# Bf16 norms, f16 feed-forward halves and new instruction orders in an attention kernel with six local layers

## The chip, the cores and the metric

One core of a Trainium2 chip runs the whole program. The metric is the device time of one execution in microseconds (us), as the median of three runs. TensorE (PE) multiplies matrices, VectorE (DVE), ScalarE (ACT) and GpSimd (POOL) work elementwise, SyncE (SP) issues all the DMAs.

## What is computed

The input is 8 batches of 512 tokens with 128 channels, in float32. First comes one causal attention with 16 heads of 64 (norm, projections, softmax over all earlier tokens, output projection, gated residual). Then six layers of local attention and feed-forward follow, of which this is the core:

```python
def attn_layer(x, Wqkv, qs, ksc, Wo):
    q, k, v = split(x @ Wqkv); q = l2norm(q) * qs; k = l2norm(k) * ksc
    q = q * cos * scale + rotate_half(q) * sin * scale      # k with 1 / scale
    out = local_attention(q, k, v)                            # windows of 32, and the window before
    return out @ Wo
def ffn_layer(x, g, bln, W1, b1, W2, b2):
    xn = (x - mu) / sqrt(var + 1e-05) * g + bln
    a, gate = split(xn @ W1 + b1)                             # 341 columns each
    return a * gelu(gate) @ W2 + b2
for i in range(6):
    x = attn_layer(shift_tokens(x), ...) + x
    x = ffn_layer(shift_tokens(x), ...) + x
```

## The kernel before, in words

The causal stage (lines L539 and the like) takes the first 670 us or so and is left almost as it is. The local stage works through 48 units, one for each layer and batch (m = 8 * layer + batch). A unit has two halves of eight heads each, v = 2m and 2m + 1. Everything is channels by tokens, 128 x 512 per tile; two such tiles side by side make a 128x1024 PSUM tile, and there are four of those: psA0, psA1, psB0 and psB1.

The steps of one half, by their names in the code: `pj` (4 of them, c = 0 to 3) projects q or k: six f16 matmuls, since x and the weights are each kept as a high and a low f16 half and three products are added. `sq` (ACT, L985) squares it, `tc` and `ts` (DVE, L1237 and L1245) multiply it by the rotary tables, `ad` (POOL, L1349 and L1350) adds these crosswise into a tile h, of which there are HN = 5, `qa` (POOL, L1354) adds the squares of the two halves of the head dimension. `ss` sums the squares over the partitions with four matmuls. The norm's inverse is made by `nr` and `ns` (ACT, L990 to L1001) and `nw` (POOL, L1357 to L1361), one Newton step on a Ln/Exp estimate. `bc` (k = 0, 1) spreads that factor to all partitions of a head by two f32 matmuls of 32 rows, `bm` (DVE, L1253) multiplies h by it, and `dm` (SP, L486) issues four DMAs for each of the four tiles, to qf and kf. `vp`, `ve` (ACT, L1007) and `vd` (SP, L502 and L504) make and copy the values. `sc` (rp = 0, 1 and t = 0 to 3) makes scores by 16 small matmuls (64 rows, 32 columns of the array), `mx` (DVE, L1257) takes their maximum, `ng` subtracts it on PE by two bf16 matmuls, `ex` (ACT, L1015) exponentiates, `tp` (L732) transposes by eight f32 matmuls, `te` (ACT, L1022) copies, `pv` (32 small matmuls each) applies them to the values, `nm` (DVE, L1266 and L1270) divides, `ot` (L758), `oe` (ACT, L1029) and `ol` (DVE, L1228) transpose and split into f16 halves.

Once a unit: `op` (24 f16 matmuls) and `rs` (DVE) are the output projection and its residual; `la`, `lb` (one f32 matmul each) with `lq`, `lw`, `lr` (ACT), `ln` (DVE) and `lx` (POOL, L1364 to L1368) are the layer norm; `f` (j = 0 to 2) is W1, two f32 matmuls of 512 columns each; `ge` (ACT, L1057) is gelu, `fm` (DVE, L1301) the product with the gate, `fo` W2 as three f32 matmuls, `fr` (DVE, L1308 and L1310) the residual with the bias b2. `xh` and `xl` split x for the next projection. Weights come once a layer (`st`, `wh`, `wl`, `oh`, `ow`; `feed_of` for W1 and W2, `tb` for the rotary tables).

Each engine works through its steps strictly in the order that the strings TENSOR, SCALAR, VECTOR, GPSIMD and SYNC write out for one unit; `walk` unrolls them, where "+1" takes a step one unit further ahead and ":A" or ":B" picks the pair of PSUM tiles. A step waits for the steps named in its code (`done`, `all_done`), and a step that takes a PSUM tile waits until the last reader of the tile's last use is through (`take`, LAST). The Gelu and the Ln/Exp functions of ACT are in different tables; `local_scalar` loads a table (L953) where a step needs another than the last one did.

## Time and profile before

| | |
|---|---|
| median of 3 runs | 3932.62 us (3932.16 to 3944.91) |
| the profiled execution's own time | 3944.91 us, the highest of the three |
| span of the profiled execution | 3944.5 us |
| busy: PE, its weight loads, DVE, ACT, POOL | 94%, 54%, 76%, 61%, 59% |
| mean granted TensorE clock | 0.983 of 2.4 GHz |

A row of the timeline gives start, duration, engine, line, operation, output<-inputs and count. Matmuls are pipelined, so what a PE step costs is the time from its start to the start of the next step and not the duration. An f32 matmul leaves two records, so "x4" of f32 is two matmuls. L677 is the helper by which nearly all local matmuls are recorded, so PE steps are told apart by their tiles.

### The profile page before, as it was taken

The numbers are of one execution on the slowest core, as the hardware profiler recorded it, in microseconds if no ns is written. First come the engines' busy times: TensorE is split into PE (matmuls) and PEld (weight loads), VectorE is DVE, ScalarE is ACT, GpSimd is POOL, SyncE is SP. The second block draws the span as 40 slices with busy tenths as digits, with TensorE's granted clock in tenths as the row PEclk, the third lists the DMA queues.
The fourth block names the chain that finished last, engine by engine and source line by source line (L and its number), as shares of the span: only waits on it lengthen the run. The fifth ranks groups of instructions, "written<-read, shape, count | busy, mean of one in ns | idle before, by whom it ended". The sixth has DMA issues, their size and how long they took to land.

```text
span 3944.5 us, 165118 instructions
## 1 busy us (share of the span) xinstructions
PE 3691.1 (94%) x73780; PEld 2146.6 (54%) x73780; DVE 2985.9 (76%) x3451; ACT 2392.9 (61%) x2931; POOL 2310.3 (59%) x1892
## 2 busy tenths in 40 slices
PE   7999998799999999999999999999999999999996
PEld 4666665455555555555555455555555555555553
DVE  7888886677777777777777677777777777777774
ACT  6777776455656655566555565555565656666652
POOL 4555654666655666656666565656565655666651
PEclk9999999899999999999999999999999999999998
DMA  1000001444444444445354444444444444444442
GB/s 59 5 5 7 5 5 39 106 100 111 101 101 104 108 108 104 101 95 123 89 121 95 97 103 108 108 107 96 109 112 109 101 101 103 110 103 106 101 101 77
DMA packets 162073, 349.17 MB, mean 89 GB/s; under 512 B 32606, under 2 KB 41948, under 8 KB 155100
## 3 DMA queue, kind: packets, MB, share of 16 engines
q1 hardware_dynamic: 161372, 338.62, 37.4%
q8 instruction: 587, 9.62, 1.0%
q14 instruction: 114, 0.93, 0.1%
HBM read 24.54 MB, written 4.19 MB: 7 GB/s over the span
## 4 chain that ended last, share of the span: by engine, by line
PE 66%; issue 5%; DMA 4%; ACT 3%; SPq 2%; DVE 2%; POOL 1%; ACTq 0%; DVEq 0%; POOLq 0%
PE psB L677 32%; PE psA L677 26%; DMA vev<-vo 3%; PE psA L732 3%; PE psB L758 2%; PE psB L732 2%; ACT pb L1015 1%; PE psA L758 1%; ACT vo L1007 1%; SPq L502 1%; SPq L486 1%; SPq L504 1%; DMA kf<-h 1%; DVE h L1253 0%; ACT sq L985 0%
## 5 line engine op out<-in xcount | busy, mean ns | idle before, releaser
L1354 POOL TENSOR_TENSOR sq<-sq 128x512 f32<-128x512 f32 x384 | 490.1, 1295 | 492.6 <-ACT sq L985 492.3
L1349 POOL TENSOR_TENSOR h<-h,ts 128x512 f32<-128x512 f32 x384 | 490.3, 1277 | 211.1 <-DVE ts L1245 211.1
L1329 POOL TENSOR_TENSOR pt<-wk,pt 128x256 f16<-128x256 f32 (+3 forms) x256 | 368.0, 1453 | 286.6 <-ACT pt L908 196.9
L1350 POOL TENSOR_TENSOR h<-h,ts 128x512 f32<-128x512 f32 x384 | 489.6, 1275 | 0.0
L985 ACT ACTIVATE sq<-psA 128x1024 f32<-128x1024 f32 x240 | 245.7, 1024 | 168.3 <-PE psA L677 168.2
L1237 DVE TENSOR_TENSOR h<-psA,t_rot 128x1024 f32<-128x1024 f32 x240 | 293.0, 1221 | 38.1 <-ACT sq L985 17.3
L677 PE MATMUL psB<-vev,ptb 64*32 64x65 f32 x9216 | 244.4, 225 | 59.0 <-ACT pb L1015 35.2
L1245 DVE TENSOR_TENSOR ts<-psA,t_rot 128x1024 f32<-128x1024 f32 x240 | 291.6, 1215 | 3.1 <-POOL h L1350 3.1
L677 PEld LDWEIGHTS psB<-vev,ptb 64*32 64x32 f32 x9216 | 194.7, 106 | 175.5 <-issue 103.3
L1364 POOL TENSOR_SCALAR f_a<-f_a 128x512 f32<-128x512 f32 x48 | 31.2, 650 | 401.6 <-DVE f_a L1293 401.6
L1253 DVE TENSOR_TENSOR h<-h,psB 128x1024 f32<-128x1024 f32 x192 | 229.5, 1217 | 42.4 <-PE psB L677 40.3
L677 PE MATMUL psB<-vo,ptb 64*32 64x65 f32 x9216 | 252.0, 226 | 6.9 <-issue 6.9
L1257 DVE TENSOR_REDUCE negm<-psA 128x16 bf16<-128x1024 f32 x96 | 117.6, 1225 | 178.9 <-PE psA L677 178.9
L1357 POOL TENSOR_TENSOR n_a<-n_s,n_a 128x512 f32<-128x512 f32 x96 | 121.9, 1269 | 192.6 <-ACT n_a L1001 192.5
L1029 ACT ACTIVATE oth<-psB 128x1024 f16<-128x1024 f32 x144 | 147.1, 1022 | 137.8 <-PE psB L758 137.5
L1253 DVE TENSOR_TENSOR h<-h,psA 128x1024 f32<-128x1024 f32 x192 | 221.3, 1215 | 5.9 <-POOL h L1350 3.7
L1270 DVE TENSOR_TENSOR ob<-psB,rc 128x512 f32<-128x512 f32 x288 | 199.3, 692 | 31.4 <-DVE rc L1266 0.9
L1237 DVE TENSOR_TENSOR h<-psB,t_rot 128x1024 f32<-128x1024 f32 x144 | 175.5, 1218 | 37.1 <-issue 35.1
L1228 DVE TENSOR_TENSOR otl<-psB,oth 128x1024 f16<-128x1024 f32 x144 | 175.3, 1218 | 27.4 <-ACT oth L1029 27.4
L1257 DVE TENSOR_REDUCE negm<-psB 128x16 bf16<-128x1024 f32 x96 | 117.2, 1221 | 103.6 <-PE psB L677 103.6
L985 ACT ACTIVATE sq<-psB 128x1024 f32<-128x1024 f32 x144 | 147.9, 1027 | 74.8 <-PE psB L677 74.8
L677 PEld LDWEIGHTS psB<-vo,ptb 64*32 64x32 f32 x9216 | 187.2, 106 | 9.1 <-issue 8.9
(343 smaller groups left out, 10637.5 us busy)
## 6 DMA issues: line engine op xcount, KB each, us to landing
qf<-h SPq DMA_DIRECT2D x768, 136.0 KB, 2.5
kf<-h SPq DMA_DIRECT2D x768, 136.0 KB
vev<-vo SPq DMA_DIRECT2D x192, 260.0 KB, 4.1
vev<-vo SPq DMA_DIRECT2D x192, 227.5 KB, 4.6
stage<-wqk SPq DMA_DIRECT2D x12, 512.0 KB, 4.6
stage<-wvl SPq DMA_DIRECT2D x12, 256.0 KB, 5.3
stage<-wof SPq DMA_DIRECT2D x6, 512.0 KB, 5.1
xb<-xt SPq DMA_DIRECT2D x8, 256.0 KB, 8.1
```

The source lines that it names most:

```text
L677: return e.matmul(o, l, r, start=start, stop=stop, skip_group_check=True, **kw)
L732: p = e.transpose(o[:, at:at + 128], pb[:, x, t, :], ident)
L985: e.activation(flat(sqb[c]), psum(("pj", v, c))[:, :], ACT.Square).then_inc(ended["sq"])
L1237: e.tensor_tensor(halves(made(v, c)), by_halves(psum(("pj", v, c))[:, :]), by_halves(flat(t_rot[:, c % 2, 0, :, :])), ALU.mult).then_inc(e ...
L1245: e.tensor_tensor(flat(tsb[i % 2]), psum(("pj", v, c))[:, :], flat(t_rot[:, c % 2, 1, :, :]), ALU.mult).then_inc(ended["ts"])
L1253: e.tensor_tensor(h, h, r.unsqueeze(1).to_broadcast([128, 2, 2, S // 2]), ALU.mult).then_inc(ended["bm"])
L1257: e.tensor_reduce(negm[rp][:, :], psum(("sc", v, rp, 0)).rearrange("p (a s) -> p a s", a=16), AXX, ALU.max, negate=True).then_inc(ended["mx"])
L1270: e.tensor_tensor(ob[:, th, :, :, :].rearrange("p q t (r d) -> p q (t r) d", d=64), o[:, :, :, 0:64], r[:, :, :].unsqueeze(3).to_broadcast ...
L1329: e.tensor_tensor(pt[g][pr][:, :, 1, o:o + w], wk[(slot_of(s)[0] - 1) % SLOTS][:, :, 0:w], pt[g][pr][:, :, 0, o:o + w], ALU.subtract).then ...
L1349: e.tensor_tensor(halves_of(h, 0), halves_of(h, 0), t[1], ALU.subtract)
L1350: e.tensor_tensor(halves_of(h, 1), halves_of(h, 1), t[0], ALU.add).then_inc(ended["ad"])
L1354: e.tensor_tensor(sqb[c][:, 0, :], sqb[c][:, 0, :], sqb[c][:, 1, :], ALU.add).then_inc(ended["qa"])
```

## The change

1. The norm factors are spread in bf16. The factor of a head stands in several rows, and each row keeps another of three bf16 pieces of it: new steps `ca`, `cb` (ACT, with a 0/1 scale per partition) and `cs`, `ct` (POOL) make them, one after the other, behind `nw`. `bc` is then two bf16 matmuls in place of two f32 ones, of the same 32 rows and 512 columns.
2. The feed-forward uses high and low f16 halves. `fh` (ACT) and `fl` (POOL) split the normed x, `gh` (ACT) and `gl` (POOL) each of the three products. `f` has six f16 matmuls in place of two f32 ones (per j), `fo` nine in place of three. The weights are split once a layer on DVE (`first_halves`, `second_halves`), behind the last `fm` and `fr` of the layer before, and for layer 0 ahead of all other local work of DVE. The bias b2 becomes a row of W2. `feed_of` is issued earlier (at u == 8 of the layer before).
3. The five order strings are new. In TENSOR the number of places where one step uses another tiling of the array than the step before it is 34.8 per unit (42.9 before, both counted from the unrolled orders). In SCALAR `ge2` stands apart from `ge1` and `ge0`, and the unrolled order has 189 table loads (95 before).

```diff
-    "vp00:A ot00:B pj10:A pj11:B sc100:B tp01:A sc101 sc102 sc103 pj13:A pj12:A ng10 pv011:B pv010:B ss1:B "
-    "sc110:A tp10:B sc111 sc112 ot01:B sc113 f1:A ng11 pv100:B f2:B f0:B pv101:A bc11:A vp10:B bc10:A tp11:B "
...
+    "sc001+1 sc003+1 ot10:B pj00:A+1 pv110:B ng00+1 pv111:B ss0:B+1 ot11:B sc010:A+1 tp00:B+1 pj11:A+1 sc012+1 "
+    "sc013+1 sc011+1 op:B pv000:B+1 ng01+1 la:B+1 bc01:B+1 pv001:A+1 lb:A+1 vp00:B+1 vp01:A+1 bc00:B+1 ot00:A+1 "
+    "pj12:A+1 tp01:B+1 pj13:B+1 pj10:A+1 fo:B pv010:A+1 ss1:B+1 pv011:B+1 vp11:B+1 f2:B+1 sc100:A+1 sc103+1 sc102+1 "
+    "sc101+1 pj02:B+2 sc110:A+1 ng10+1 vp10:B+1 sc113+1 sc112+1 sc111+1 bc10:B+1 ot01:A+1 tp10:B+1 ng11+1 bc11:B+1 "
+    "pv100:B+1 pv101:A+1 pj03:A+2 f1:B+1 f0:A+1 pj01:B+2 tp11:A+1 sc000:A+2 sc002+2 "
...
+    "ca1+1 sq02+2 oh cb1+1 ex10+1 ve10+1 oe01+1 wh1+1 te10+1 ex11+1 sq03+2 ge1+1 ge0+1 sq01+2 te11+1 gh1+1 gh2+1 "
+    "oe10+1 sq00+2 ex00+2 nr0+2 oe11+1 ns0+2 tb1+2 sq11+2 gh0+1 te00+2 ca0+2 cb0+2 ex01+2 lq+2 lw+2 lr+2 ve00+2 "
+    "ve01+2 oe00+2 sq12+2 fh+2 te01+2 sq13+2 sq10+2 wh0+2 nr1+2 ns1+2 xh+3 ve11+2 ge2+2 "
...
+    "nm001+1 bm03+1 ln+1 bm00+1 bm01+1 ol00+1 tc12+1 ts12+1 tc13+1 ts13+1 fr wl0+1 tc10+1 nm011+1 ts10+1 nm010+1 "
+    "mx10+1 fm2+1 tc02+2 ts02+2 mx11+1 bm11+1 bm10+1 ol01+1 bm12+1 bm13+1 nm101+1 nm100+1 tc03+2 ts03+2 fm0+1 fm1+1 "
+    "ow tc01+2 wl1+1 ts01+2 mx00+2 ol10+1 nm110+1 nm111+1 tc00+2 ts00+2 ol11+1 tc11+2 ts11+2 mx01+2 rs+1 nm000+2 "
+    "bm02+2 "
...
+    "ad11+1 gl0 qa11+1 lx+1 qa12+1 fl+1 qa13+1 qa10+1 ad12+1 ad13+1 nw1+1 cs1+1 ct1+1 ad10+1 ad02+2 qa02+2 xl+2 "
+    "qa03+2 ad03+2 gl1+1 qa01+2 gl2+1 qa00+2 ad01+2 ad00+2 nw0+2 cs0+2 ct0+2 "
...
+    "dm13 vd1 st0 dm02+1 dm03+1 dm01+1 dm00+1 st1 vd0+1 dm11+1 dm10+1 dm12+1 "
...
-                    e.wait_ge(*done("nw", v))
+                    e.wait_ge(*done("ct", v))
...
-                        p = mm(o[:, 512 * x:512 * x + 512], spread[rows, :], n_a[rows, :], tile_position=(64 * k + 32 * x, 0))
+                        p = mm(o[:, 512 * x:512 * x + 512], spread[rows, :], n_b[rows, :], tile_position=(64 * k + 32 * x, 0))
...
-                        p = mm(o[0:n, 512 * x:512 * x + 512], w1r[:, FF * x + 128 * j:FF * x + 128 * j + n], f_c[:, :])
+                        mm(oy, w1s[1][:, at:at + n], f_ch[:, :], True, False)
+                        mm(oy, w1s[0][:, at:at + n], f_cl[:, :], False, False)
+                        p = mm(oy, w1s[0][:, at:at + n], f_ch[:, :], False, True)
...
-                        p = mm(o[:, 0:512], w2r[0:n, j, :], f_g[j][0:n, :], j == 0, j == 2)
+                        mm(o[:, 0:512], w2s[1][0:n, j, :], f_gh[j][0:n, :], j == 0, False)
+                        mm(o[:, 0:512], w2s[0][0:n, j, :], f_gl[j][0:n, :], False, False)
+                        p = mm(o[:, 0:512], w2s[0][0:n, j, :], f_gh[j][0:n, :], False, j == 2)
...
+                elif kind == "ca":
+                    e.wait_ge(*done("nw", v))
+                    e.activation(n_c[:, :], n_a[:, :], ACT.Copy, scale=less[:, 0:1]).then_inc(ended["ca"])
+                elif kind == "cb":
+                    e.wait_ge(*done("cs", v))
+                    e.activation(n_c[:, :], n_a[:, :], ACT.Copy, scale=less[:, 1:2]).then_inc(ended["cb"])
...
+                elif kind == "fh":
+                    if v:
+                        e.wait_ge(*all_done("f", *((v - 1, j) for j in range(3))))
+                    e.wait_ge(*done("lx", v))
+                    e.activation(f_ch[:, :], f_c[:, :], ACT.Copy).then_inc(ended["fh"])
...
+            first_halves(e, 0)
+            second_halves(e, 0)
...
+                elif kind == "cs":
+                    e.wait_ge(*done("ca", v))
+                    e.tensor_tensor(n_a[:, :], n_a[:, :], n_c[:, :], ALU.subtract).then_inc(ended["cs"])
+                elif kind == "ct":
+                    if v:
+                        e.wait_ge(*all_done("bc", (v - 1, 0), (v - 1, 1)))
+                    e.wait_ge(*done("cb", v))
+                    e.tensor_tensor(n_b[:, :], n_a[:, :], n_c[:, :], ALU.subtract).then_inc(ended["ct"])
...
+                    e.tensor_tensor(f_gl[j][0:n, :], f_g[j][0:n, :], f_gh[j][0:n, :], ALU.subtract).then_inc(ended["gl"])
```

## Rows read from the trace of the kernel before

**Rows 1.** Stretches: start:end, length, busy PE, PEld, DVE, ACT, POOL; clock, DMA, GB/s

```profile
1254.10:1644.80 390.70, 376.96 (x8022) 215.81 (x8018) 298.22 (x342) 234.63 (x272) 241.79 (x205) 1.00 0.47 107
...
1112.00:1254.10 142.10, 129.01 (x2669) 72.72 (x2670) 103.95 (x116) 85.09 (x103) 82.05 (x69) 0.98 0.43 99
```

**Rows 2.** Chain that ended last: an `op` step, six units before 1644.75

```profile
1254.13 5.29 PE psB L677 x24
```

**Rows 3.** Timeline of PE, f32 and small matmuls of one unit

```profile
995.34 1.12 PE L677 MATMUL psA<-f_a,t_mats 128*128 128x512 f32 x2
996.40 0.25 PE L677 MATMUL psB<-vev,ptb 64*32 64x65 f32 x2
...
997.19 1.13 PE L677 MATMUL psB<-n_a,t_mats 32*128 32x512 f32 x4
998.24 0.30 PE L677 MATMUL psA<-wvth,xs0l 128*64 128x256 f16 x2
...
999.68 1.09 PE L758 MATMUL psB<-t_mats,ob 128*128 128x128 f32 x8
1000.61 0.38 PE L677 MATMUL psA<-xs1h,wql 128*128 128x512 f16 x1
...
1001.90 0.38 PE L677 MATMUL psB<-xs1h,wql 128*128 128x512 f16 x1
...
1003.29 0.39 PE L677 MATMUL psB<-t_masks 64*128 64x128 bf16 x4
...
1014.11 0.39 PE L677 MATMUL psA<-t_masks 64*128 64x128 bf16 x4
1014.44 0.45 PE L677 MATMUL psA<-kf,qf 64*32 64x64 f32 x32
1014.82 1.09 PE L732 MATMUL psB<-t_mats,pb 128*128 128x128 f32 x8
```

**Rows 4.** Timeline of PE: `f` and `fo`, with the steps behind them

```profile
1018.65 1.98 PE L677 MATMUL psA<-f_c,w1r 128*128 128x512 f32 x4
1020.47 0.59 PE L677 MATMUL psA<-negm,t_masks 128*128 128x512 bf16 x2
1021.00 0.25 PE L677 MATMUL psB<-vev,ptb 64*32 64x65 f32 x2
...
1509.88 2.85 PE L677 MATMUL psB<-f_g,w2r 128*128 128x512 f32 x6
1512.65 1.06 PE L677 MATMUL psA<-sq,t_mats 128*32 128x512 f32 x8
```

**Rows 5.** Groups by line and form: like operations; count, busy us, mean ns

```profile
L953 ACT ACT_TABLE_LOAD x95 | 121.9, 1283 | 1.7
L977 ACT ACTIVATE t_rot<-t_tab,t_scl 128x512 f32<-128x512 f32 x48 | 30.0, 715 | 0.0
L1341 POOL TENSOR_TENSOR xs1l<-xb,xs1h 128x512 f16<-128x512 f32 x24 | 27.3, 1136 | 0.0
```

**Rows 6.** Timelines of ACT and POOL: the norm chain and like operations

```profile
1477.62 0.63 ACT L960 ACTIVATE xs1h<-xb 128x512 f16<-128x512 f32 x1
1480.03 0.69 ACT L990 ACTIVATE n_s<-psB,t_eps 128x512 f32<-128x512 f32 x1 [1.78 <-PE psB L677]
...
1482.93 0.63 ACT L1001 ACTIVATE n_a<-n_r 128x512 f32<-128x512 f32 x1
1483.81 1.02 ACT L1029 ACTIVATE oth<-psB 128x1024 f16<-128x1024 f32 x1 [0.25 <-PE psB L758]
...
1484.17 1.29 POOL L1357 TENSOR_TENSOR n_a<-n_s,n_a 128x512 f32<-128x512 f32 x1
...
1486.26 1.27 POOL L1361 TENSOR_TENSOR n_a<-n_a,n_r 128x512 f32<-128x512 f32 x1
```

**Rows 7.** Timelines of SP and DVE at the start of the local stage

```profile
680.54 0.33 SPq L527 DMA_DIRECT2D w1r<-w  x1
...
683.19 1.16 DVE L1237 TENSOR_TENSOR h<-psA,t_rot 128x1024 f32<-128x1024 f32 x1
```

More of the change, by code:

```diff
@@ L24 @@
 FP = [128, 128, FF - 256]
+FK = [128, 128, FF - 255]
 NEG = -1e30
@@ L27 @@
 WS = 64.0
+WF = 8.0
 TINY = WS * WS * 1e-24
@@ L203, in walk, with with_first @@
     return out, rings
+def with_first(steps, *first):
+    return list(first) + [s for s in steps if s not in first]
 def ordinals(walks):
@@ L316, in program @@
         n_r, n_a = (sb("n_" + x, [128, S]) for x in "ra")
+        n_c, n_b = (sb("n_" + x, [128, S], BF16) for x in "cb")
         vo = [sb(f"vo{n}", [128, 8, 4, 65]) for n in range(2)]
@@ L326, in program @@
         f_g = [sb(f"f_g{j}", [128, S]) for j in range(3)]
+        f_ch, f_cl = (sb("f_c" + z, [128, S], F16) for z in "hl")
+        f_gh, f_gl = ([sb(f"f_g{z}{j}", [128, S], F16) for j in range(3)] for z in "hl")
+        w1s = [sb("w1" + z, [128, 2 * FF], F16) for z in "hl"]
+        w2s = [sb("w2" + z, [128, 3, 128], F16) for z in "hl"]
+        t_gs = sb("t_gs", [128, L])
         x1d = nc.dram_tensor("x1_keep", [NB, 128, S], F32).ap()
@@ L342, in program @@
         s_wa = sems("s_wa", 3)
-        s_const, s_first, s_ct, s_x, s_wo, s_wm, s_w1, s_w2, s_tab, s_stage, s_x1r = (
-            sem("s_" + n) for n in ("const", "first", "ct", "x", "wo", "wm", "w1", "w2", "tab", "stage", "x1r"))
+        s_const, s_first, s_cin, s_x, s_wo, s_wm, s_w1, s_w2, s_tab, s_stage, s_x1r = (
+            sem("s_" + n) for n in ("const", "first", "cin", "x", "wo", "wm", "w1", "w2", "tab", "stage", "x1r"))
         s_dm = sems("s_dm", 4)
@@ L508, in sync @@
                     heads_of(e, li + 1, 0)
-                if u == 2 and li:
-                    e.wait_ge(*all_done("f", *((NB * li - 1, j) for j in range(3))))
-                    e.wait_ge(*done("fo", NB * li - 1))
-                    feed_of(e, li)
+                if u == 8 and li + 1 < L:
+                    e.wait_ge(*done("lb", NB * li))
+                    e.wait_ge(s_w1s, li + 1)
+                    e.wait_ge(s_w2s, li + 1)
+                    feed_of(e, li + 1)
             e.wait_ge(*done("ss", 2 * NB * L - 1))
@@ L1038, in local_scalar @@
                     if v:
-                        e.wait_ge(*all_done("f", *((v - 1, j) for j in range(3))))
+                        e.wait_ge(*done("fl", v - 1))
                     e.wait_ge(*done("la", v))
@@ L1206, in weights_low, with first_halves, second_halves @@
                                    ).then_inc(ended["wl"])
+        def first_halves(e, li):
+            e.wait_ge(s_w1, 16 * (li + 1))
+            g = t_gs[:, li:li + 1]
+            e.tensor_scalar(w1s[0][:, :], w1r[:, :], g, None, ALU.mult).then_inc(s_w1h)
+            e.wait_ge(s_w1h, li + 1)
+            e.scalar_tensor_tensor(out=w1s[1][:, :], in0=w1r[:, :], scalar=g, in1=w1s[0][:, :], op0=ALU.mult,
+                                   op1=ALU.subtract).then_inc(s_w1s)
+        def second_halves(e, li):
+            e.wait_ge(s_w2, 48 * (li + 1))
+            for j in range(3):
+                n = FK[j]
+                e.tensor_scalar(w2s[0][0:n, j, :], w2r[0:n, j, :], WF, None, ALU.mult).then_inc(s_w2h)
+            e.wait_ge(s_w2h, 3 * li + 3)
+            for j in range(3):
+                n = FK[j]
+                p = e.scalar_tensor_tensor(out=w2s[1][0:n, j, :], in0=w2r[0:n, j, :], scalar=WF, in1=w2s[0][0:n, j, :],
+                                           op0=ALU.mult, op1=ALU.subtract)
+            p.then_inc(s_w2s)
         def local_vector(e):
@@ L1255, in local_vector @@
                     rp = s[2]
-                    e.wait_ge(*done("sc", v, rp, NT - 1))
+                    e.wait_ge(*all_done("sc", *((v, rp, t) for t in range(NT))))
                     e.tensor_reduce(negm[rp][:, :], psum(("sc", v, rp, 0)).rearrange("p (a s) -> p a s", a=16), AXX, ALU.max,
```

117 lines of the change are left out of this document (70 added, 47 removed), and 6 rows, old and new, of tables (TENSOR, VECTOR).

## The prediction

> **What bounds the kernel now.** I read the stretches of time first. Between 1254.1 and 1644.8 us, exactly six units of the local stage, PE is busy for 377.0 of 390.7 us, DVE for 298.2, POOL for 241.8 and ACT for 234.6 [rows 1]. Per unit that is 65.1 us, with PE at 62.8, DVE 49.7, POOL 40.3, ACT 39.1. The reader is to see that PE alone is full: it idles 2.3 us a unit, and the next engine has 15 us to spare. Second I read the chain of waits: it runs from one PE step to the next, and the 24 matmuls of `op` in it cost 5.29 us [rows 2]. So, in steady units, a microsecond taken from PE shortens the unit until its idle time grows. There are 48 units, and all that is said per unit is taken 48 times. Third I read the timeline of PE, for the price of each step from its start to the next start.
>
> **What PE is spared.** `bc` now takes 1.05 us (997.19 to 998.24) for two f32 matmuls of 32 rows [rows 3]. `lb`, one f32 matmul of 512 columns, takes 1.06 (995.34 to 996.40) [rows 3]: the two of `bc` run side by side. In bf16, bounds are the price of one 16-bit matmul of 512 columns, 0.215 (six in `pj` from 1000.61 to 1001.90 [rows 3]), and of two in a row, 0.53 (`ng`, 1020.47 to 1021.00 [rows 4]). I take 0.27, near the lower end, since the same two tiles run side by side in f32. That spares 0.78, four times a unit: 3.1 us. `f` costs 1.82 (1018.65 to 1020.47) [rows 4] and becomes six matmuls of 0.215, 1.29: 0.53 less, three times, 1.6 us. `fo` costs 2.77 (1509.88 to 1512.65) [rows 4] and becomes nine, 1.94: 0.83 less. Together 5.5 us.
>
> The new order of TENSOR has 8.1 fewer places per unit where the tiling changes. A `pj` ahead of another `pj` costs 1.29 and one ahead of small score matmuls 1.39 (1001.90 to 1003.29) [rows 3], so each change is worth 0 to 0.1. I take 0.09, the nearest row's: 0.7 us. PE then has 6.2 us a unit less to do, 56.6 in place of 62.8.
>
> A rule speaks against the first of these terms. In the trace the f32 `bc` with a change of tiling on both sides costs no more than `lb`, 1.05 against 1.06 [rows 3]. The Trainium skill, TensorEngine Tiling (Array Packing), Key Properties, says that a change of tiling mode drains TensorE, which a short `bc` could hide less well than a long one. By the row the term stays at 0.27; by the rule, with a drain at both ends, it would lie near the upper bound of 0.53.
>
> **What the others get.** ACT: `ca` and `cb` at 0.72 (with a scale per partition, as L977 [rows 5]), four a unit, 2.9; `fh` and three `gh` at 0.63 (as L960 [rows 6]), 2.5; and about two more table loads a unit at 1.28 [rows 5], because `ge2` stands alone, 2.6. Sum 8.0: ACT goes from 39.1 to 47. POOL: `cs` and `ct` at 1.14 to 1.29 (L1341 [rows 5], L1357 [rows 6]), four, 4.8; `fl` and three `gl` at 1.14, 4.6. Sum 9.4: POOL from 40.3 to 50. DVE gets four small instructions and the weights' halves once a layer, some 2 to 3 us per 8 units: 50. All of this is hidden by PE's 56.6 as long as nobody waits for it; without that cover ACT's and POOL's 17 us would be on the path. Of DMAs nothing is added but one row of W2; `feed_of` with its four issues is moved to u == 8 once a layer, behind steps that were done long before.
>
> **What becomes late.** The norm chain from `ss` to `bc` gets four links in a row on two engines. For `ss1` it is: `nr` and `ns` 3.53 (1480.03 to 1483.56), then `nw` 3.36 (1484.17 to 1487.53) [rows 6]. Meanwhile ACT, in its order, does `xh`, `ve11`, a table load and `ge2`, 0.63 + 1.02 + 1.28 + 0.69 = 3.62, and only then `ca`; so the chain is 3.53 + 3.62 + 0.72 + 1.2 + 0.72 + 1.2 = 11.0. Five hand-offs between engines come to it, each between 0 and 0.25 (the idle time ahead of `oth` [rows 6]): 11.0 to 12.3. PE's steps between `ss1` and `bc10` in the new string, priced from [rows 3, 4] (`pv` 0.79, `vp` 1.44, `f` 1.29, `sc` 0.38, with its masks 0.71, `pj` 1.29, `ng` 0.53), come to 10.5. PE stalls for 0.5 to 1.8; I take 1.1. Behind the waiting `bc10` stand `ot01`, `tp10` and all of PE. For `ss0` the cover is 12.7 (`op` is in it), the chain 0.69 + 1.02 + 2.84 + 3.36 + 3.84 = 11.8 and hand-offs: no stall. The rest is queueing: PE's idle time of 2.3 us a unit can stay, or double as ACT and POOL fill up and covers such as `ng11` plus `bc11` for `te10` (0.80 against 1.02) fall short. Bounds 0 and 2.3; I take 0.9. Net per unit: 6.2 - 1.1 - 0.9 = 4.2 us.
>
> **Start and end.** Ahead of its first `tc`, at 683.19, DVE now waits for W1 and W2, issued from 680.54 [rows 7], and makes eight instructions: 0 to 8 us, I take 5. The first norm chain has no cover and is longer by `ca` to `ct`, 3.8 or 4. At the end `fh`, `fl`, `gh`, `gl` stand bare, 0.63 + 1.14 twice, against shorter `f` and `fo`: 2 to 3. Sum 12 us more, and the causal stage as before.
>
> **The sum.** The profiled execution's own time is 3944.9 us, 12.3 above the median of the three runs. 3944.9 - 48 x 4.2 + 12 = 3755, and 12 less against the median: **3743 us**. Its own bounds: stalls of 0.5 + 0 give 3944.9 - 48 x 5.7 + 12 - 12 = 3671, stalls of 1.8 + 2.3 give 3844.
>
> **Rivals.**
> *All is covered.* The new orders lose nothing, hand-offs and queues included: 48 x 6.2, 3647 us. For it: DVE, the next engine, would be at 50 of 58.9. Against it: the 10.5 us cover above, shorter than the chain. Chance 0.10.
> *The clock.* With 56.6 of 60.9 us PE would be busy for 93% of the time. The steady stretch has 96% and a granted clock of 1.00; the stretch with 129.0 of 142.1 us, 91%, has 0.98 [rows 1], which means 4% of the time at 1.2 GHz in place of 2.4. At 0.98 everywhere a unit loses 2%, 1.2 us: 3743 + 58 = 3801. Against it: the drops there may come from the layer's change alone. Chance 0.12. The Trainium skill, TensorE: Matmul & The Clock Gate, HAM oscillation, says that idle gaps between bursts of matmuls make the clock fall; the trace agrees in direction, with these two stretches.
> *The change does less than it says.* The two bf16 matmuls of `bc` run one after the other, 0.53 in place of 0.27: 0.26 x 4 x 48 = 50, 3793 us. Chance 0.06.
> *Slower: the norm chain is the new bound.* Each of the four new links waits in its engine's order behind one instruction of another step, 1.02 to 1.29, some 4.6 a half. The chains are then 16.9 and 16.2 against covers of 12.7 and 10.5, stalls of 9.9 a unit, and the unit is 6.2 - 9.9 - 0.9, 4.6 us longer: 3932.6 + 221, about 4150 us. It decides from the point where both stalls and the queueing together pass 6.2 us. For it: ACT and POOL are strict in order and go from 39 and 40 to 47 and 50 us. Against it: `cb` stands straight behind `ca` or one step off, `cs` straight behind `nw`. Chance 0.09. With half of that queueing gain and loss cancel, near 3933: chance 0.05.
>
> **The numbers.** The forecast itself has 0.58. The range reaches to the clock, the serial `bc` and part of the full cover, 3660 to 3860, which leaves out the last two cases and half of the first. A measurement of this kernel can tell about 0.5% from no change. Faster by more than that: 0.58 + 0.10 + 0.12 + 0.06 = 0.86; the same 0.05; slower 0.09.
>
> **What would show it.** In the profile after: `bc` from start to start near 0.27, `f` 1.29, `fo` 1.94; PE's busy time per steady unit near 56.6 and a unit near 61; table loads 189; ACT near 47, POOL near 50 us a unit; waits of PE for the bf16 norm (n_b) of about 1 us a unit, at `bc10` and not at `bc01`; the first `tc` some 5 us later. The prediction is wrong if PE waits for n_b by 3 us or more a unit, if the clock in steady units is under 0.99, or if another engine's idle time is under 3 us a unit.

## The result, and the profile after

The changed kernel takes **3875.07 us** (median of four runs, 3865.54 to 3887.12) against 3932.39 for the kernel before, run beside it (3930.80 to 3944.91). The ratio is 0.9846 [0.9822, 0.9871]: 57 us faster, where 189 were forecast. The profiled execution took 3872.99 us with a span of 3870.9, 73.6 below the span before.

First the page of the changed kernel: busy time by engine, the granted clock in 40 slices, and the chain that ended last.

```profile
PE 3467.5 (90%) x73828; PEld 2108.7 (54%) x73828; DVE 3028.9 (78%) x3502; ACT 2713.0 (70%) x3409; POOL 2762.1 (71%) x2276
...
PEclk9999999799999999999999999999999999999997
...
PE 44%; DVE 11%; POOL 10%; issue 10%; ACT 6%; SPq 1%; DMA 1%; DVEq 0%; ACTq 0%; POOLq 0%
```

PE has lost 224 us of busy time (94% of the span before, 90% now), but the span only 74. The chain before ran through PE for 66% of the span; now it leaves PE for DVE, POOL and ACT in more than a quarter. The kernel is no longer bound by PE alone.

Next the stretches of time, with the columns of [rows 1]. First the kernel before, from the first `op` of the local stage to the last (47 units), then its sixth and seventh unit, where a layer changes:

```profile
787.16:3898.59 3111.43, 2959.51 (x62505) 1687.03 (x62495) 2333.04 (x2665) 1854.26 (x2161) 1869.16 (x1572) 0.99 0.46 104
1111.93:1182.57 70.64, 64.62 (x1344) 36.55 (x1334) 52.80 (x58) 40.23 (x48) 42.58 (x35) 0.98 0.42 95
1182.57:1254.07 71.50, 64.42 (x1346) 36.21 (x1335) 51.16 (x58) 44.90 (x56) 39.51 (x34) 0.98 0.43 102
```

And the kernel after: the same 47 units, four undisturbed units of the last layer, one unit behind the change to the fourth layer, and the unit in which the first layer changes to the second:

```profile
792.17:3816.30 3024.13, 2735.76 (x62417) 1645.78 (x62413) 2371.51 (x2704) 2164.77 (x2624) 2303.82 (x1943) 0.98 0.46 107
3521.36:3764.60 243.24, 228.37 (x5340) 138.02 (x5335) 197.35 (x224) 181.75 (x220) 196.78 (x167) 1.00 0.48 109
2355.86:2424.85 68.99, 60.66 (x1354) 36.57 (x1348) 55.64 (x67) 46.04 (x56) 50.07 (x43) 0.95 0.42 96
1170.39:1246.19 75.80, 63.95 (x1340) 37.29 (x1336) 52.04 (x59) 53.67 (x68) 51.18 (x44) 0.89 0.44 105
```

The sums close. Over 47 units PE is busy for 223.8 us less (2959.51 - 2735.76) and idle for 136.5 us more (288.4 against 151.9), so the stage is 87.3 shorter. It starts 5.0 us later (792.17 against 787.16), and behind its last `op` come 54.6 us in place of 45.9: 87.3 - 5.0 - 8.7 = 73.6. The best units are as forecast: 243.24 / 4 = 60.8 us, against 60.9 worked out. But few are like that. I cut the trace at the starts of `op`, took the granted clock of each of the first 46 units, and sorted them by whether it is full:

```
                       units of full clock            units below it
                     n    unit   PE busy  idle     n    unit   clock
before              35   65.09    62.88   2.21    11   70.60   0.965
after               28   62.15    57.50   4.66    18   68.45   0.943
```

In units of full clock the change saves 2.94 us, not 4.2: PE's work falls by 5.38 and its idle time grows by 2.45. And seven more units are disturbed.

The prices of the steps, from PE's timeline in one unit of the last layer: `bc`, `fo`, and one `f`, each with its next step.

```profile
3529.32 0.39 PE L675 MATMUL psB<-n_b,t_masks 32*128 32x512 bf16 x2
3529.64 0.25 PE L675 MATMUL psA<-vev,ptb 64*32 64x65 f32 x2
...
3540.26 0.38 PE L675 MATMUL psB<-f_gh,w2l 128*128 128x512 f16 x1
...
3541.99 0.38 PE L675 MATMUL psB<-f_gh,w2h 86*128 86x512 f16 x1
3542.30 0.25 PE L675 MATMUL psA<-vev,ptb 64*32 64x65 f32 x2
...
3559.27 0.39 PE L675 MATMUL psB<-n_b,t_masks 32*128 32x512 bf16 x2 [0.32 <-DVE h L1302]
...
3562.66 0.39 PE L675 MATMUL psB<-f_ch,w1l 128*128 128x512 f16 x1
...
3563.96 0.38 PE L675 MATMUL psA<-f_ch,w1l 128*128 128x512 f16 x1
```

`bc` costs 0.32 (3529.64 - 3529.32), `fo` 2.04 (3542.30 - 3540.26), `f` 1.30 (3563.96 - 3562.66): they answer to [rows 3, 4]. The last `bc` of these rows has waited 0.32 for its PSUM tile, which `bm` (L1302) still read. PE's waits between 1254 and 3800 us show who it now waits for; the columns are the sum, the number and the longest of the waits.

```profile
PE psA L675 <- issue: 74.9, 58, 3.0
PE psB L675 <- DVE ob L1319: 31.5, 9, 5.8
PE psB L675 <- DVE h L1302: 25.1, 39, 1.0
PE psB L675 <- ACT n_s L994: 18.0, 4, 6.2
...
PE psB L675 <- POOL n_b L1420: 3.5, 4, 1.1
```

Three things are to be seen. The norm chain, which I took for the main new wait, makes 3.5 us in all 39 units of this stretch. Then there are waits for other engines of two kinds: many short ones, like the one for DVE's `bm` (L1302), once a unit and at most 1.0 us, and four or nine long ones of up to 6 us, once or twice a layer. And the largest row of all is "issue": idle time for which the profile names nobody. With the rows of the other tiles it is 86.7 us, against 51.2 in the same stretch of the kernel before, whose rows are these:

```profile
PE psA L677 <- issue: 30.8, 17, 4.0
...
PE psB L677 <- issue: 20.4, 30, 1.6
```

Most of it stands in the middle of a step, ahead of a matmul that waits for no semaphore, as here, two matmuls before the end of `sc`:

```profile
2055.27 0.69 PE L675 MATMUL psA<-kf,qf 64*32 64x64 f32 x48
2058.37 0.30 PE L675 MATMUL psA<-kf,qf 64*32 64x64 f32 x2 [2.41 <-issue]
2058.60 0.39 PE L675 MATMUL psB<-xs1h,wql 128*128 128x512 f16 x1
```

I call these *instruction gaps*, for what the trace says of them. Between 790 and 3800 us the changed kernel has 83 of over 0.15 us (48 before). From each to the next it is a multiple of 125.9 matmuls, within 5 matmuls, in all 82 cases (47 of 47 before); with their weight loads and semaphore steps that is 256 or 257 records of PE's stream. The page's row for the DMA queue that brings instructions,

```profile
q8 instruction: 588, 9.63, 1.0%
```

has 588 packets of 16 KB, and the 150,526 records of PE are 588 lots of 256. And each of the 83 gaps ends 1.2 to 1.7 us behind the landing of such a packet, where one in nine of all matmul starts does. So in these gaps PE waits for its own instructions.

### The profile page after: what moved, and what is told of

Read it like the earlier page. It is cut to its first block, busy times and chain, and to the rows that moved or that the text cites. A ratio compares the mean times of both kernels' runs of the same rounds, so it can differ in the third digit from the quotient of the medians.

```text
span 3870.9 us, 166364 instructions
## 1 busy us (share of the span) xinstructions
PE 3467.5 (90%) x73828; PEld 2108.7 (54%) x73828; DVE 3028.9 (78%) x3502; ACT 2713.0 (70%) x3409; POOL 2762.1 (71%) x2276
## 4 chain that ended last, share of the span: by engine, by line
PE 44%; DVE 11%; POOL 10%; issue 10%; ACT 6%; SPq 1%; DMA 1%; DVEq 0%; ACTq 0%; POOLq 0%
PE psB L675 22%; PE psA L675 17%; POOL sq L1405 2%; DVE h L1302 2%; POOL h L1400 2%; POOL h L1401 2%; PE psB L730 2%; ACT sq L989 2%; PE psB L756 1%; PE psA L756 1%; POOL f_gl L1437 1%; DVE h L1286 1%; SPq L483 1%; DVE ts L1294 1%; DVE xb L1327 1%
## 5 line engine op out<-in xcount | busy, mean ns | idle before, releaser
L1302 DVE TENSOR_TENSOR h<-h,psB 128x1024 f32<-128x1024 f32 x384 | 455.8, 1214 | 57.4 <-PE psB L675 51.5
L675 PE MATMUL psA<-kf,qf 64*32 64x64 f32 x24576 | 323.2, 229 | 68.8 <-issue 68.8
L675 PEld LDWEIGHTS psA<-kf,qf 64*32 64x32 f32 x24576 | 266.1, 107 | 151.7 <-issue 151.0
L1306 DVE TENSOR_REDUCE negm<-psA 128x16 bf16<-128x1024 f32 x192 | 234.0, 1219 | 142.6 <-PE psA L675 142.3
L1023 ACT ACTIVATE pb<-psA 128x1024 f32<-128x1024 f32 x192 | 196.7, 1025 | 63.5 <-PE psA L675 62.4
L1286 DVE TENSOR_TENSOR h<-psB,t_rot 128x1024 f32<-128x1024 f32 x144 | 176.2, 1224 | 73.7 <-ACT sq L989 39.4
L675 PE MATMUL psB<-vev,ptb 64*32 64x65 f32 x7680 | 200.8, 225 | 34.0 <-ACT ptb L1030 13.9
L1437 POOL TENSOR_TENSOR f_gl<-f_g,f_gh 128x512 f16<-128x512 f32 x144 | 174.8, 1215 | 55.2 <-ACT f_gh L1078 55.2
L675 PE MATMUL psB<-vo,ptb 64*32 64x65 f32 x7680 | 207.1, 226 | 2.3 <-issue 2.3
L1415 POOL TENSOR_TENSOR n_a<-n_a,n_c 128x512 f32<-128x512 f32 x96 | 111.0, 1156 | 123.3 <-ACT n_c L1006 123.3
L1420 POOL TENSOR_TENSOR n_b<-n_a,n_c 128x512 bf16<-128x512 f32 x96 | 111.3, 1159 | 120.9 <-ACT n_c L1009 120.9
```

The source lines that it names most:

```text
L675: return e.matmul(o, l, r, start=start, stop=stop, skip_group_check=True, **kw)
L1286: e.tensor_tensor(halves(made(v, c)), by_halves(psum(("pj", v, c))[:, :]), by_halves(flat(t_rot[:, c % 2, 0, :, :])), ALU.mult).then_inc(e ...
L1302: e.tensor_tensor(h, h, r.unsqueeze(1).to_broadcast([128, 2, 2, S // 2]), ALU.mult).then_inc(ended["bm"])
L1306: e.tensor_reduce(negm[rp][:, :], psum(("sc", v, rp, 0)).rearrange("p (a s) -> p a s", a=16), AXX, ALU.max, negate=True).then_inc(ended["mx"])
L1437: e.tensor_tensor(f_gl[j][0:n, :], f_g[j][0:n, :], f_gh[j][0:n, :], ALU.subtract).then_inc(ended["gl"])
```

## The experiments

The ratios are to the kernel before, run beside each; "us" is the ratio's distance from 1 times 3932. Each edit was made to the kernel named.

### Where a layer changes, and the table loads

Layer 0's weights and rotary tables were kept for all six layers, in the kernel before and in the changed one:

```diff
-                ok = 0 <= s[1] < 2 * L * NB and s[1] % (2 * NB) == 0
+                ok = s[1] == 0
...
-                if u == 6 and li + 1 < L:
+                if False:
```

> The kernel before, with the weights, rotary tables and feed-forward weights of layer 0 kept for all six layers: no reloads, no splits, no rescaling at a layer's end (this leaves out the other layers' weights). Theory A (what I missed is the change of layer): before, two units per layer were 5 to 6 us longer than the rest, so 5 x 11 = 55 us go, about 3880 us, all units near 65.0. Theory B (the steady units are what I misjudged): the same here, it only sets the scale for the next kernel.

> The changed kernel with the weights of layer 0 kept for all layers, in the same way. Theory A: the layer's change disturbs more units than two, and with it gone all units are as in the last layer, near 60.8 us: 792 + 47 x 60.8 + 55 = about 3705 us, 170 less than the changed kernel. Theory B (queueing behind fuller ACT and POOL): only the two long units go, the rest stay at 62.5 to 63: about 3790 us, 85 less.

Measured: 0.9866 [0.9843, 0.9890] and 0.9611 [0.9586, 0.9636]. The change of layers costs 53 us before, and 0.9846 - 0.9611 or 92 us after: some 39 us of the miss (each ratio is good to about 10 us). The rest of the miss is still there without it: 3791 us is theory B's number, and 16 units stay below full clock.

Gelu was replaced by Identity, so that one table serves ACT throughout, in both kernels:

```diff
-                needs = {"ge": "gelu_and_others"}.get(kind, "natural_log_exp_and_others")
+                needs = "natural_log_exp_and_others"
```

> The kernel before with Identity in place of Gelu, so that no ACT table load is left (95 gone; the values of the feed-forward are others). ACT is 60% busy here: all theories expect no change over 0.5%, 3915 to 3940 us.

> The changed kernel with Identity in place of Gelu: 189 table loads of 1.28 us gone. Theory B (ACT's order is where PE's waits begin): 1 to 2 us a unit, 3875 - 50 to 100 = 3775 to 3825 us. Theory A (layer change): under 20 us less, 3855 to 3875.

Measured: 0.9991 [0.9978, 1.0003] and 0.9893 [0.9873, 0.9912]. All of the 189 loads that the profile after has are gone,

```profile
L957 ACT ACT_TABLE_LOAD x189 | 242.5, 1283 | 3.3
```

ACT has 5.2 us a unit less to do (46.6 to 41.4), and neither kernel is faster. The second is even slower than the changed kernel, by 18 us (0.9893 against 0.9846), which both theories missed; why, no run shows. So no time of the changed kernel can be put down to the loads.

In the changed kernel the second half's weights were fetched ahead of the DMAs of `dm` in SYNC:

```diff
-    "dm13 vd1 st0 dm02+1 dm03+1 dm01+1 dm00+1 st1 vd0+1 dm11+1 dm10+1 dm12+1 "
+    "dm13 vd1 st0 st1 dm02+1 dm03+1 dm01+1 dm00+1 vd0+1 dm11+1 dm10+1 dm12+1 "
```

> The changed kernel with st1, the load of the second half of the next layer's weights, moved in SP's order ahead of the four dm steps. In the trace of the changed kernel ACT waited 5.9 us for that load once a layer, DVE 4.9 us behind it, and pv on PE took 5.4 in place of 0.8 us. Theory A: 5 to 8 us a layer, 5 times, 25 to 40 us faster: 3835 to 3850. Theory B: the wait passes to the next in the queue, under 15 us.

Measured: 0.9827 [0.9800, 0.9854], which the interval doesn't tell from 0.9846: theory B. The aim came from these rows of ACT and DVE in the changed kernel, at the first change of layers:

```profile
1169.98 4.99 ACT L981 ACTIVATE t_rot<-t_tab,t_scl 128x512 f32<-128x512 f32 x8
...
1202.70 1.06 ACT L947 ACTIVATE wqh<-stage 128x1024 f16<-128x1024 f32 x1 [5.92 <-DMA stage<-wvl]
```

```profile
1175.96 1.23 DVE L1286 TENSOR_TENSOR h<-psA,t_rot 128x1024 f32<-128x1024 f32 x1 [7.32 <-ACT sq L989]
...
1204.31 1.23 DVE L1223 SCALAR_TENSOR_TENSOR wql<-stage,wqh 128x1024 f16<-128x1024 f32 x1 [4.89 <-ACT wvth L948]
```

The eight scalings of the rotary tables hold up ACT for 5.0 us, so DVE is idle for 7.3; some 27 us later the weights come late and both wait again. Taking the second wait away shortened the unit in which the layer changes from 73.7 to 71.5 us on average (the first from 75.8 to 70.9), and others grew.

### One part of the change at a time, under the new orders

The norm part was undone (`bc` in f32 from `nw`'s result, `ca`, `cb`, `cs`, `ct` gone from the strings), then the feed-forward part (f32 `f` and `fo`, the weights fetched at u == 1 and 3, no halves), then both, which leaves the new orders with the old arithmetic:

```diff
-                    e.wait_ge(*done("ct", v))
+                    e.wait_ge(*done("nw", v))
...
-                        p = mm(o[:, 512 * x:512 * x + 512], spread[rows, :], n_b[rows, :], tile_position=(64 * k + 32 * x, 0))
+                        p = mm(o[:, 512 * x:512 * x + 512], spread32[rows, :], n_a[rows, :], tile_position=(64 * k + 32 * x, 0))
```

> The changed kernel with the norm spread in f32 again (bc as before, no ca, cb, cs, ct), all else and the orders as changed. My forecast: bc costs 1.06 again, 0.74 us more four times a unit, against about 1 us of norm-chain stall that goes, so 48 x 2 = 95 us slower than the changed kernel, 3970. Theory B (ACT and POOL are full, in-order waits eat the gain): their 7.7 us a unit less gives most of it back, 3860 to 3900 us.

> The changed kernel with the feed-forward in f32 again (no fh, fl, gh, gl, no split weights; W1 and W2 fetched at u == 1 and 3 since this order needs W1 earlier), norms and orders as changed. My forecast: f and fo cost 2.4 us a unit more on PE, 115 us slower than the changed kernel: 3990. Theory A (the weights' splits at the layer's end disturb it): 5 x 5 to 10 us come back, 3940 to 3965. Theory B: ACT gets 2.5 and POOL 4.6 us a unit back, 3900 to 3930.

> The changed kernel's order strings alone: norms and feed-forward in f32 as in the kernel before, none of the new steps. PE, ACT, DVE and POOL have the work of the kernel before. Theory O: the order itself costs, 4000 to 4070 us (the single undone parts cost 129 and 46 us on the changed kernel). Theory Q: without the new steps it is as good as the old order, 3920 to 3960 us.

Measured: 1.0178 [1.0147, 1.0208], 0.9967 [0.9952, 0.9982] and 1.0156 [1.0139, 1.0173]. From the changed kernel's 0.9846 the norm part is worth 130 us and the feed-forward part 48, where the forecast's terms have 149 and 115. For the norm 3970 us was my forecast and 4014 measured; for the feed-forward it was 3990, and 3930 came, the upper edge of theory B. The two don't add up: together they are worth 122 us (1.0156 - 0.9846), and with the norm in f32 the feed-forward part is worth nothing (1.0178 and 1.0156, whose intervals overlap). The new orders with the old arithmetic cost 61 us, as theory O had it.

Then the steps that make the pieces and halves were taken out of the changed kernel, while PE's work stayed: `nw` writes its result straight in bf16, `lx` and `fm` in f16, and the smaller pieces are left out.

```diff
-                    e.tensor_tensor(n_a[:, :], n_a[:, :], n_r[:, :], ALU.mult).then_inc(ended["nw"])
+                    e.tensor_tensor(n_b[:, :], n_a[:, :], n_r[:, :], ALU.mult).then_inc(ended["nw"])
```

> The changed kernel with its matmuls and order as they are, but without the splitting steps: nw writes its result as bf16 straight into the tile that bc reads, lx and fm write f16 high halves, the low halves are zero (left out: two of the three pieces of the norm, the low halves of the feed-forward). ca, cb, cs, ct, fh, fl, gh, gl are gone: 8 us less work on ACT and 9.5 on POOL per unit, the same on PE. Theory Q (the new steps of ACT and POOL make PE wait): the unit falls from 62.5 to about 60, 3740 to 3780 us. Theory O (the new order of PE stalls by itself, whatever ACT and POOL do): under 40 us faster, 3835 to 3875.

Measured: 0.9802 [0.9782, 0.9823], 17 us faster than the change, in theory O's range. ACT and POOL fall back to 41.9 and 40.6 us a unit (46.6 and 49.8 in the changed kernel), and PE's idle time in units of full clock only from 4.66 to 4.12 us. So of the 13.9 us of ACT and POOL work a unit that are gone, 0.5 stood in PE's idle time; the rest was hidden. That the two engines are fuller isn't the main cause.

### The same work under the old orders

> The same arithmetic as the last kernel (no splitting steps, low parts zero), with the order strings of the kernel before. PE's work is 5.3 us a unit less than before and nothing is added elsewhere. Theory O: the old order keeps the gain, a unit of 60, about 3690 us. Theory Q: the same as the last kernel within 40 us, 3740 to 3780.

Measured: 0.9680 [0.9660, 0.9700], the fastest kernel of the study with all layers' weights, 65 us faster than the change. Theory O's 3690 us isn't reached (3810 measured), and it is above theory Q's range too, though the old orders are the better ones here. (Its arithmetic is less: the smaller pieces are zero.) Even so PE is spared 4.5 us in a unit of full clock and the unit shrinks by 2.6.

Now the full new arithmetic in the old orders, `ca` to `ct`, `fh` to `gl` put in by hand where their inputs are ready:

```diff
-    "lx qa10 ad10 qa11 qa13 qa12 ad11 xl+1 ad13 nw1 ad12 qa01+1 ad01+1 ad00+1 qa00+1 qa03+1 qa02+1 ad03+1 nw0+1 "
-    "ad02+1 "
+    "lx qa10 ad10 fl qa11 qa13 qa12 ad11 xl+1 ad13 nw1 cs1 ct1 ad12 gl1 gl2 gl0 qa01+1 ad01+1 ad00+1 qa00+1 "
+    "qa03+1 qa02+1 ad03+1 nw0+1 cs0+1 ct0+1 ad02+1 "
```

> The changed kernel's arithmetic in full, with the order strings of the kernel before and the new steps put in by hand where their inputs come (ca0 behind tb1, cb0 behind te00, ca1 behind te10, cb1 behind oh, fh behind te01, gh behind te11, cs and ct behind nw, fl behind ad10, gl behind ad12). Theory O: the old order was better for PE, 3780 to 3850 us. Theory Q: without a new order the steps are later still, 3900 to 3980 us.

Measured: 1.1057 [1.1039, 1.1076], 416 us slower, which neither theory had. Its profile shows the rival that I had called slower, the norm chain as the new bound: the chain through POOL, and PE's waits between 1254 and 3800 us.

```profile
PE 31%; POOL 27%; ACT 10%; issue 8%; DVE 7%; SPq 0%; DMA 0%; ACTq 0%; DVEq 0%; POOLq 0%
```

```profile
PE psB L674 <- POOL n_b L1419: 151.7, 34, 8.6
PE psA L674 <- DVE f_g L1347: 65.5, 34, 1.9
PE psA L674 <- ACT pb L1022: 59.0, 34, 2.4
```

A unit waits 4.5 us for `ct` at one place (151.7 / 34), 1.9 for `fm`, whose L1347 stands ahead of `gh`. All 46 units fall below full clock (0.92 on average), so a unit of 75 us is also slow in its matmuls. With the steps put in at these places the old orders can't carry the new arithmetic: 4356 against 3875 us. Other places weren't tried.

Which part needs them? The feed-forward part alone, put in by hand in the old orders:

> The old orders with the feed-forward part of the change alone, its fh, fl, gh, gl put in by hand; norm as before. It tells which of the two parts needs the new orders, and whether a version with less of the change beats both kernels. PE is spared 0.5 three times and 0.2 to 0.8 in fo, about 2 us a unit. If the feed-forward chain is covered in the old order, and half of the saving turns into time as in the run with the cheap matmuls and old orders: 48 x 1.0, about 3890 us, 0.988. If the chain is exposed as in the run with both parts put in by hand (82 us of waits for the gate's product in 34 units, 2.4 a unit, and 80 for the exponentials): 3940 + 48 x 2.7 = 4070 us, 1.03, and then the norm part made only the smaller half of that run's 415 us.

Measured: 1.0055 [1.0036, 1.0074], 22 us slower than before, 3955 us and so between the two forecasts. So, if the two parts add up here, some 390 of the 416 us come in with the norm part; that part alone wasn't run in the old orders.

### Who PE runs into

In the changed kernel and in the fastest one, `ol` was cut to 8 of 64 columns, which takes 4 us a unit from DVE alone:

```diff
-                    e.tensor_tensor(lo, psum(("ot", v, rp))[:, :].rearrange("p (h q n) -> p h q n", h=2, q=2), hi,
+                    e.tensor_tensor(lo[:, :, :, 0:8], src[:, :, :, 0:8], hi[:, :, :, 0:8],
```

> The changed kernel, in which ol (DVE, 1.22 us, four a unit) subtracts only 8 of every 64 columns; the rest of the low halves of the attention output stays zero and is left out of the result. DVE has about 4 us a unit less to do, PE, ACT and POOL the same. It asks whether PE's idle time of 4.7 us in the undisturbed units is time in which DVE is behind. Theory D (DVE's queue is what PE catches up with, now that PE is shorter: about 92 of the 233 us of waits in the stretch from 1254 to 3800 us are put down to DVE): the idle time falls by 1.5 to 2 us a unit, about 3785 us, 0.962 of before. Theory O (many short covers, each a hand-off's length, whichever engine makes it; the new order fixes them): no more than 0.5% from the changed kernel, 3855 to 3880 us, 0.98.

> The same cut of ol in the kernel with the old orders and the cheap matmuls, whose low halves are left out (3810 us, unit 62.5 with 58.4 busy in units of full clock). Only DVE is made lighter, by about 4 us of 50. Theory D: DVE and what hangs on it made half of the saved PE time come back as idle time, so the unit shrinks by 2 us, about 3720 us, 0.945 of before. Theory O: 3800, within 0.5% of the run without the cut, since its waits for ACT (29 us), for the copies by DMA (18) and for POOL (17) remain.

Measured: 0.9843 [0.9827, 0.9859] and 0.9689 [0.9673, 0.9704]; without the cut they are 0.9846 and 0.9680. DVE is at 46.0 in place of 50.0 us a unit in the second, and nothing moves. Theory D has fallen: no full queue of DVE stands behind PE's idle time. Of PE's waits between 1254 and 3800 us, the fastest kernel has these; the first line stands as good as unchanged beside the kernel before, the others are new or larger.

```profile
PE psB L674 <- ACT pb L1022: 29.0, 39, 1.1
...
PE psA L674 <- DVE ts L1294: 19.1, 37, 1.2
PE psB L674 <- DMA vev<-vo: 17.6, 22, 1.4
PE psA L674 <- POOL sq L1407: 16.5, 32, 0.6
```

The kernel before had for the same stretch:

```profile
PE psB L677 <- ACT pb L1015: 28.3, 38, 1.0
...
PE psB L677 <- DMA vev<-vo: 12.6, 21, 1.4
...
PE psB L677 <- POOL sq L1354: 0.3, 1, 0.3
```

The wait at `ss`, behind `fo`, is the case in point: with its nine short matmuls done, PE comes to it about half a microsecond before the PSUM tile is free, as two rows below show. Before, the f32 `fo` covered that.

Which of PE's savings turns into time? In the old orders, the norm alone and the feed-forward alone were made cheap (the same edits as above, one at a time):

> The old orders and the old feed-forward; only bc is made cheap, by writing the norm factor straight as one bf16 value (the two smaller pieces are left out, so no ca, cb, cs, ct). PE is spared 0.74 four times a unit, 142 us in 48 units. Theory T (the time that PE is spared at bc is turned into time, that in the feed-forward is not, since f and fo stand between their own chain's links): about 3937 - 130 = 3807 us, 0.967, as fast as the run with both. Theory H (half of any saving comes back as idle time): 3865 us, 0.982.

> The old orders and the old norm; only the feed-forward matmuls are f16, with the low halves of the normed x and of the three products left out and their high halves written directly (no fh, fl, gh, gl). PE is spared 0.45 three times and 0.2 at fo, some 1.6 us a unit, 77 us. Theory T: no change, 3925 to 3945 us, 1.00. Theory H: 3895 us, 0.99. Against the run with fh, fl, gh and gl put in by hand (1.0055) it also gives the price of these steps without an order made for them.

Measured: 0.9816 [0.9796, 0.9836] and 0.9878 [0.9861, 0.9895]: 72 and 48 us, 120 together, and 126 were measured for both at once. Theory H's numbers (3865 and 3895 us) are met with 3865 and 3889, theory T falls. By units of full clock:

```
                       unit   PE busy   idle
before                65.09    62.88    2.21
norm cheap            63.74    60.18    3.56
feed-forward cheap    64.26    61.15    3.11
both cheap            62.50    58.39    4.11
```

One place of this is seen in two rows of PE's timeline, of the kernel with the feed-forward cheap (the last matmul of `fo`, then `ss`):

```profile
2884.90 0.38 PE L674 MATMUL psB<-f_gh,w2h 86*128 86x512 f16 x1
2885.75 1.06 PE L674 MATMUL psA<-sq,t_mats 128*32 128x512 f32 x8 [0.47 <-DVE ts L1296]
```

`fo` begins at 2883.16, so to `ss` it is 2.59 us, against 2.77 with f32 [rows 4]: of the 0.7 us by which the f16 `fo` is shorter, 0.47 are a wait for `ts`, the last reader of the PSUM tile.

PE's work falls by 2.70, 1.73 and 4.49, its idle time grows by 1.35, 0.90 and 1.90. In these three kernels 42 to 52% of what PE is spared comes back as idle time. In the changed kernel it is 46% (2.45 of 5.38), but there it isn't the same idle time. The table takes the instruction gaps out of it, for units of full clock:

```
                                  PE busy   idle   instruction gaps   the rest
before                              62.88   2.21               0.88       1.33
old orders, both cheap              58.39   4.11               0.97       3.14
new orders, old arithmetic          61.94   2.67               1.61       1.06
new orders, cheap, no pieces        57.32   4.12               2.10       2.02
changed kernel                      57.50   4.66               2.40       2.26
```

In the old orders nearly all of the growth (1.81 of 1.90) is waiting for other engines. In the changed kernel that is 0.93 of 2.45; the other 1.52 are gaps in which PE waits for its instructions, and 0.73 of them are there with the old arithmetic, so they come with the new orders. A likely reason is in the TENSOR string: it has the four `sc` of a tile back to back, two runs of 128 small matmuls a unit, where before but one run in the whole kernel was longer than 96. 55 of the 83 gaps stand in such a run, 34 of them behind at least 80 of its matmuls (before: 26 of 48, and 6). Shorter runs in the new orders weren't tried.

### What the new orders cost

The new orders with the old arithmetic, and layer 0's weights kept:

> The new orders with the old arithmetic (4000 us with all weights), in which layer 0's weights and rotary tables are kept for all six layers: nothing is fetched, split or scaled after the first layer, so the result of layers 1 to 5 is another. To be compared with the kernel before under the same cut (0.9866 of before, 3890 us). Theory L (the new orders stall PE where a layer changes, not in the other units: in units of full clock they need 64.6 us against 65.1, and only 27 units in place of 35 have full clock): the 62 us that the new orders cost vanish, about 3870 to 3890 us, 0.985. Theory S (their stalls are spread over all units): 3890 + 62 = 3952 us, 1.002.

Measured: 0.9897 [0.9872, 0.9921], against 0.9866 for the old orders under the same cut. Of the 61 us that the new orders cost with the old arithmetic, 12 are left, and the two intervals overlap: nearly all of it goes with the change of layers, as theory L had it. Its stretch from the first `op` to the last, beside the same orders with all weights and two of that kernel's units at a change of layers:

```profile
791.54:3844.49 3052.95, 2899.41 (x62367) 1697.61 (x62366) 2311.81 (x2634) 1902.72 (x2184) 1868.05 (x1568) 0.99 0.45 102
```

```profile
789.98:3946.14 3156.16, 2939.85 (x62366) 1713.84 (x62365) 2337.50 (x2664) 1947.07 (x2250) 1872.94 (x1569) 0.97 0.44 103
...
1179.28:1257.54 78.26, 68.21 (x1340) 38.07 (x1335) 51.36 (x58) 47.22 (x58) 40.48 (x35) 0.89 0.42 98
1257.54:1330.31 72.77, 63.77 (x1340) 37.37 (x1335) 50.82 (x57) 41.93 (x49) 41.45 (x35) 0.95 0.41 100
```

In units of full clock these orders are half a microsecond better than the old ones (64.61 against 65.09: 0.94 less of PE's work, 0.46 more idle time). Their loss is at the change of layers, where the two units take 78.3 and 72.8 us in place of 70.6 and 71.5. In the first of them PE is busy for 68.2 us, 4.4 more than in the next one, at a granted clock of 0.89 against 0.95: part of the price of the stall is paid in slower matmuls.

The one-layer runs also show what comes ahead of the falls of the clock in the other units. For every fall of the granted clock from 2.4 to 1.2 GHz between 792 and 3740 us I looked for PE's longest idle gap in the 8 us ahead of it:

```
weights of one layer        falls   behind an instruction gap   its length
before                          2                           2   1.6 and 2.0 us
new orders, old arithmetic      8                           8   1.8 to 2.6 us
changed kernel                 19                          17   1.7 to 2.6 us
```

Of the changed kernel's 20 instruction gaps of 2.0 us or more in this run, 14 are followed by a fall. With all weights the changed kernel has 25 falls, and 20 of them come behind a wait for another engine or a DMA, of up to 6.2 us; the fastest kernel has no instruction gap over 1.5 us and 12 falls, all behind waits of 1.4 to 4.6 us.

## Why the prediction was wrong

The direction was right, and PE's prices nearly. The miss, between the two profiled executions, is 118 us (189.6 less were worked out, 71.9 came), and nearly all of it lies in the 47 units.

**PE bound, and its microseconds are worth a microsecond.** The sentence "so, in steady units, a microsecond taken from PE shortens the unit until its idle time grows" holds; what I missed is that its idle time grows at once. **This is the first step that failed**: "PE's idle time of 2.3 us a unit can stay, or double as ACT and POOL fill up ... I take 0.9". It went from 2.21 to 4.66, the bound of 2.3 and a little more, and for other reasons than the one given. ACT and POOL filling up is 0.5 of it (4.66 against 4.12 without the pieces; the two causes below contain it), DVE's queue nothing. Two causes stand in its place. PE's order is laced with hand-offs that its own steps cover by a few tenths of a microsecond, and the covers shrink with the steps: 1.81 us in the old orders, where nothing was added, 0.93 in the changed kernel. And 1.52 us are instruction gaps, which no term had; half of them come with the new orders alone.

**The norm chain.** I took 1.1 us a unit of stall at `bc10`. The four links take what was worked out, 0.72 or 1.16 us each with hand-offs under 0.15, but PE's waits for n_b come to 3.5 us in 39 units, 0.1 each. This term was mis-sized by nearly its whole amount. That the two errors cancel in part is luck: 2.45 us of idle time together, where 2.0 were forecast, 21 us in 47 units.

**PE's work.** 5.4 us a unit less in place of 6.2. On average over the units of full clock, from start to start without the waits, `bc` costs 0.35 (1.06 before), `f` 1.36 (1.87) and `fo` 1.96 (2.77): 5.2 of the 5.5 us. The other steps together give 0.2 of the 0.7 that I took for the tiling changes: `tp` is 0.28 shorter and `vp` 0.12, but `op` 0.11 longer (5.30 in place of 5.19), `ng` 0.12 and `pv` 0.15. With the old arithmetic the same orders spare PE 0.94, 0.35 of it at `tp`, so the term was no overestimate there. This is 39 us of the miss in 47 units. Of the rule of the Trainium skill, TensorEngine Tiling (Array Packing), Key Properties, that a change of tiling drains TensorE: `bc` has other tilings before and behind it and costs 0.32 in the rows, near the lower bound of 0.27 and not 0.53. By the row the rule leaves no more than 0.05 us over what I took, by the average 0.08.

**"All that is said per unit is taken 48 times."** This is **the second step that failed**, and as dear as the others: the units aren't alike. The excess of the disturbed ones over the units of full clock was 61 us before (11 x 5.5) and is 113 now (18 x 6.3), 52 us that stood in no term. The runs with one layer's weights put 39 of it down to the change of layers. I had priced what is moved there (`feed_of`, the halves of the weights) by its busy time and not asked what stands behind it in ACT's and DVE's order. The rest goes with the clock in ordinary units: 16 of 46 units stay below full clock without any change of weights, where the kernel before has 2, and 17 of the 19 falls come behind an instruction gap. (With all weights the number of such units isn't exact: the changed kernel's one profile has 18, that of the kernel with the short `ol`, which takes the same time, 22.)

**The rivals.** The clock (3801 us, chance 0.12) was partly true, as part of the disturbed units, and of the prediction's signs of being wrong it is the one that came (0.988 on average over the 46 units of the changed kernel with one layer's weights). I can't give it a number of its own: a stall comes with each fall. The Trainium skill, TensorE: Matmul & The Clock Gate, A second HAM failure mode: psum-queue depth-cycling, says that short idle gaps between groups of matmuls, as PSUM tiles are cycled, already make the clock fall. The traces agree in part: the change has twice the idle time and seven more units below full clock, but the fastest kernel, with 4.1 us of idle time a unit, has 10 such units against 11 before. The sum of idle time doesn't decide it; what differs is the single gap, as the falls behind instruction gaps show. That `bc` might run serially is excluded. "All is covered" fell on the order's short covers and on the instruction gaps. The slow rival, the norm chain as the bound, is real: it came in the old orders with the steps put in by hand, where PE's largest single wait, 4.5 of 12.2 us of idle time a unit, is for `ct`.

**ACT, POOL, start and end.** ACT 46.6, POOL 49.8, DVE 51.0 us a unit, as forecast (47, 50, 50), hidden but for 17 us of the whole time. The table loads are 189, and no time is gained without them. The start is 5.0 us later in place of 9 (the first `tc` 1.5 in place of 5), the end 8.7 longer in place of 2 to 3; without the split steps the end is 45.5 us again, so they stand bare there for more than I gave them. In sum 13.7 against 12.

**What stays open.** How much of the disturbed units is clock and how much stall; whether new orders with shorter runs of `sc` would have fewer instruction gaps; and why the kernel without table loads is slower. An order string made for the cheap steps without the pieces wasn't tried.

## What to carry to other kernels

When the bounding engine's steps get shorter, don't credit the whole saving even if the next engine has 15 us to spare: its steps are also the cover of every hand-off in its order, and in the old orders of this kernel 42 to 52% of what PE was spared came back, mostly as waits of half a microsecond. List the hand-offs with their margin before and subtract the new step lengths, rather than follow only the chain that gets longer. Read "issue" rows like any other wait: gaps in the middle of a step that lie a fixed number of instructions apart are the engine waiting for its program, and long runs of tiny matmuls are where they stood here. And count the units that aren't like the others apart: a new order is judged at the change of layers too, not in the steady unit alone.
